# A perceiver stack on one core: products of the second attention in three reduced-precision passes, with changes to its loads, to a block inversion and to the self-attention

## The reference

```python
x = x + _L0_xattn_ref(...)  # attention over the context with a bias, 16 heads, then a feed-forward
x = x + _L0_attn_ref(...)   # delta-rule memory: per head and chunk of 64 the inverse of a unit triangular matrix
x = x + _L0_ffn_ref(...)    # eight dense gated experts, all of them summed
x = x + _L1_xattn_ref(...)  # second attention over the context, 16 heads of 64
x = x + _L1_attn_ref(...)   # self-attention over 64 tokens, 16 heads of 16
x = x + _L1_ffn_ref(...)    # eight experts, one picked per token
```

```python
q = x @ Wq
kv = context @ Wkv
k, v = jnp.split(kv, 2, axis=-1)
...
sim = jnp.einsum('bhid,bhjd->bhij', q, k) * scale
sim = jnp.where(mask[None, None, :, :], sim, max_neg)   # j % n_q == i: 16 of 1024 keys for each query
attn = jax.nn.softmax(sim, axis=-1)
out = jnp.einsum('bhij,bhjd->bhid', attn, v)
```

## Time and profile before

| what | value |
|---|---|
| median of 3 runs | 879.33 us (878.36 to 882.39) |
| the profiled execution's own time | 886.54 us |
| its span, first to last instruction | 884.7 us |
| mean granted TensorE clock | 0.986 |
| TensorE busy, matmuls | 832.1 us, 94% |
| VectorE busy | 511.5 us, 58% |
| ScalarE busy | 414.7 us, 47% |
| GpSimd busy | 97.4 us, 11% |

### The profile page before, as it was taken

How to read it: one execution, slowest core, us unless ns; L and a number is a source line. 1 busy time by engine, 2 the same in 40 slices (tenths; PEclk the granted TensorE clock), 3 DMA queues, 4 the chain that set the end, 5 groups by cost and what they waited for, 6 DMA issues and landing times.

```text
span 884.7 us, 20345 instructions
## 1 busy us (share of the span) xinstructions
PE 832.1 (94%) x8172; PEld 671.4 (76%) x8172; DVE 511.5 (58%) x1226; ACT 414.7 (47%) x852; POOL 97.4 (11%) x96
## 2 busy tenths in 40 slices
PE   7999999999889798999999999999998899879997
PEld 5888888888747796888888888887368757668785
DVE  6777887777646646555555555555246524575332
ACT  4666656666652224445445454443456632522221
POOL 1323320340000520000000000000000000400100
PEclk9999999999999799999999999999999999899999
DMA  8445654485090000123113213003617768033960
GB/s 315 178 138 202 235 213 159 135 285 199 5 399 1 3 4 2 43 101 142 69 75 142 86 57 142 0 0 141 239 49 282 282 248 333 1 147 115 367 235 25
DMA packets 26017, 128.19 MB, mean 145 GB/s; under 512 B 2376, under 2 KB 8416, under 8 KB 21856
## 3 DMA queue, kind: packets, MB, share of 16 engines
q1 hardware_dynamic: 24624, 110.83, 33.7%
q0 software_dynamic: 1328, 16.41, 4.8%
HBM read 126.71 MB, written 0.52 MB: 144 GB/s over the span
## 4 chain that ended last, share of the span: by engine, by line
PE 78%; DVE 9%; DMA 7%; issue 3%; ACT 2%; SPq 1%; DVEq 0%
PE PS L461 13%; PE PS L463 13%; PE PS L462 13%; PE PS L766 4%; PE PS L1220 3%; DMA arena<-in_bias 3%; PE PS L887 3%; PE PS L1232 3%; DMA hT<-in_ctxD 3%; PE PS L778 3%; PE PS L755 3%; PE PS L1034 2%; PE PS L481 2%; PE PS L1000 2%; PE PS L355 2%
## 5 line engine op out<-in xcount | busy, mean ns | idle before, releaser
L1401 ACT CAST w_h<-arena 128x768 fp32r<-128x768 f32 x64 | 53.4, 835 | 124.8 <-PE PS L463 124.8
L1755 DVE TENSOR_TENSOR w_l<-arena,w_h 128x768 fp32r<-128x768 f32 x64 | 61.2, 958 | 87.1 <-ACT w_h L1401 87.0
L461 PE MATMUL PS<-xnT_h,w_h 128*128 128x512 f32 x256 | 99.7, 389 | 1.4 <-DVE xnT_l L455 1.4
L463 PE MATMUL PS<-xnT_h,w_l 128*128 128x512 f32 x256 | 99.6, 389 | 0.0
L462 PE MATMUL PS<-xnT_l,w_h 128*128 128x512 f32 x256 | 99.6, 389 | 0.0
L1600 DVE CUSTOM_DVE_ANT_0 arena<-PS,arena 128x512 f32<-128x512 f32 x128 | 86.9, 715 | 19.9 <-PE PS L755 17.8
L1299 ACT ACTIVATE arena<-arena 128x1024 f32<-128x1024 f32 x64 | 73.5, 1150 | 10.8 <-DVE arena L1600 10.7
L766 PE MATMUL PS<-consts,arena 128*128 128x128 f32 x512 | 68.3, 277 | 0.7 <-ACT arena L1304 0.4
L766 PEld LDWEIGHTS PS<-consts,arena 128*128 128x128 f32 x512 | 55.9, 141 | 10.5 <-issue 3.6
L1762 DVE TENSOR_TENSOR arena<-PS,arena 128x512 f32<-128x512 f32 x64 | 44.3, 692 | 29.0 <-PE PS L463 27.3
L461 PEld LDWEIGHTS PS<-xnT_h,w_h 128*128 128x128 f32 x256 | 48.1, 188 | 11.6 <-DVE xnT_l L455 1.8
(11 more groups left out here) (312 smaller groups left out, 1736.0 us busy)
## 6 DMA issues: line engine op xcount, KB each, us to landing
arena<-in_bias SPq DMA_DIRECT2D x64, 512.0 KB, 4.1
arena<-in_wall SPq DMA_DIRECT2D x8, 3072.0 KB, 10.5
arena<-in_wf SPq DMA_DIRECT2D x8, 2052.0 KB, 11.2
hT<-in_ctxT SPq DMA_DIRECT2D x8, 1024.0 KB, 5.7
arena<-in_ctxD SPq DMA_DIRECT2D x4, 1024.0 KB, 7.6
arena<-in_ctxG SPq DMA_DIRECT2D x4, 1024.0 KB, 4.7
hT<-in_ctxD SPq DMA_DIRECT2D x4, 1024.0 KB, 8.2
hT<-in_ctxG SPq DMA_DIRECT2D x4, 1024.0 KB, 4.9
```

Of the source, the lines that this page charges most:

```text
L461: pe.matmul(out, a[0], b[0], start=start, stop=False)
L463: return pe.matmul(out, a[1], b[0], start=False, stop=stop)
L1401: act.copy(w_h[:, s % 4, :], stage[s // 8 % 2][:, s % 8, :]).then_inc(sem("c_wh"), 1)
L1755: dve.tensor_tensor(w_l[:, s % 4, :], stage[s // 8 % 2][:, s % 8, :], wide(w_h[:, s % 4, :]), ALU.subtract).then_inc(sem("c_wl"), 1)
```

## The change

The change merges several edits.

1. **Second attention.** Query weights and key weights are loaded while the dense experts still run, and GpSimd splits them (eight instructions). The normalised tokens are split on arrival. Queries and `U` are formed in three fp32r passes; ScalarE writes `qs_h`, VectorE the new `qs_l`.
2. **Contexts.** Three buffers instead of two. `wv1` and `wo1` are loaded after `U` is complete, ahead of context 3; the self-attention's weights and the last block's first five expert blocks after the product with `wv1` (before: earlier). The warming matmuls ahead of the batch loop go from 8 to 2.
3. **Inversion.** VectorE makes `T`, `MT` and `CT[1]` for two heads at a time; `TT` comes from TensorE (a product with the identity) and a ScalarE copy; GpSimd keeps the later masks alone.
4. **Self-attention.** The values of the second four batches are formed behind the first two tiles' scores; ScalarE takes over one of two value copies of VectorE and its last turned copy; `weighted` uses one bank for each tile, and `output` divides tile by tile.

```diff
+            w_in(wq1, A["wq1"], "in_wq1")
+            w_in(wkT1, A["wkT1"], "in_wq1")
 
             sp.wait_ge(sem("c_dn"), 4 + 8 * NEXP)
-            w_in(wq1, A["wq1"], "in_wq1")
-            w_in(wkT1, A["wkT1"], "in_wk1")
-            w_in(wv1, A["wv1"], "in_wvo1")
-            w_in(wo1, A["wo1"], "in_wvo1")
             for b in range(B):
-                if b >= 2:
-                    sp.wait_ge(sem("d_sim"), 2 * (b - 1))
...
+                if b == 3:
+                    for dc in range(KC):
+                        sp.wait_ge(sem(f"d_u{dc}"), 2 * FC)
+                    w_in(wv1, A["wv1"], "in_wvo1")
+                    w_in(wo1, A["wo1"], "in_wvo1")
+                if b >= 3:
+                    sp.wait_ge(sem("d_sim"), 2 * (b - 2))
+                sp.dma_start(ctxT1[b % 3], A["ctxD"][b].rearrange("(k p) n -> p k n", p=P))\
+                  .then_inc(sem(f"d_ctxT{b % 3}"), 16)
+                if b >= 3:
+                    sp.wait_ge(sem("d_w"), 4 * (b - 2))
+                sp.dma_start(ctxG[b % 3], A["ctxG"][b]).then_inc(sem(f"d_ctxG{b % 3}"), 16)
+            sp.wait_ge(sem("d_o"), FC)
             w_in(wqkv, A["wqkv"], "in_wqkv")
             w_in(wproj, A["wproj"], "in_wqkv")
...
-            for h in range(MH):
-                pool.wait_ge(sem("b_t"), h + 1)
-                pool.tensor_tensor(TT[:, h], MT[:, h], masked("up0"), ALU.mult).then_inc(sem("b_pool"), 1)
-                pool.wait_ge(sem("b_pool"), 2 * h + 1)
-                pool.tensor_tensor(TT[:, h], masked("pick64"), TT[:, h], ALU.subtract).then_inc(sem("b_pool"), 1)
+            pool.wait_ge(sem("b_ct"), MH)
...
+            pool.wait_ge(sem("in_wq1"), 32)
+            n = 0
+            for raw, high, low in ((wq1, wq1_h, wq1_l), (wkT1, wkT_h, wkT_l)):
+                half = raw.shape[1] // 2
+                for k in (slice(0, half), slice(half, 2 * half)):
+                    pool.tensor_copy(high[:, k], raw[:, k]).then_inc(sem("d_ws"), 1)
+                    n += 2
+                    pool.wait_ge(sem("d_ws"), n - 1)
+                    pool.tensor_tensor(low[:, k], raw[:, k], wide(high[:, k]), ALU.subtract).then_inc(sem("d_ws"), 1)
...
                     if k == 1:
+                        pe.wait_ge(sem("b_copied"), 3 + h)
+                        for t in range(NT):
+                            for r in halves:
+                                last = pe.matmul(PS[r, 4 + h, t * S:(t + 1) * S], T[r, h, t, :], C("pick64")[r],
+                                                 start=True, stop=True)
+                        last.then_inc(sem("b_x"), 1)
                         pe.wait_ge(sem("b_ct"), h + 1)
...
+            pe.wait_ge(sem("tr_l"), 4 * KC)
+            pe.wait_ge(sem("d_ws"), 4)
 
             def q_mm(c):
                 if c >= 2:
-                    pe.wait_ge(sem("d_qs"), c - 1)
+                    pe.wait_ge(sem("d_ql"), c - 1)
                 for ki in range(KC):
-                    last = pe.matmul(bank(c % 2), wq1[:, ki, c * P:(c + 1) * P], xnT[:, ki],
-                                     start=ki == 0, stop=ki == KC - 1)
+                    w = slice(c * P, (c + 1) * P)
+                    last = mm3(pe, bank(c % 2), (wq1_h[:, ki, w], wq1_l[:, ki, w]), (xnT_h[:, ki], xnT_l[:, ki]),
+                               ki == 0, ki == KC - 1)
...
                 for dc in range(KC):
-                    for h2 in range(2):
-                        if c:
-                            pe.wait_ge(sem(f"d_ue{dc}"), 2 * (c - 1) + h2 + 1)
-                        r = slice(64 * h2, 64 * h2 + 64)
-                        pe.matmul(bank(2 + 2 * h2 + dc), wkT1[r, c, dc * P:(dc + 1) * P], qs1[r, c % 2, :],
-                                  start=True, stop=True).then_inc(sem(f"d_u{dc}"), 1)
+                    if c:
+                        pe.wait_ge(sem(f"d_ue{dc}"), 2 * c)
+                    for n, (w, q) in enumerate(((wkT_h, qs_h), (wkT_h, qs_l), (wkT_l, qs_h))):
+                        for h2, r in enumerate(halves):
+                            last = pe.matmul(bank(2 + 2 * h2 + dc), w[r, c, dc * P:(dc + 1) * P], q[r, c % 2, :],
+                                             start=n == 0, stop=n == 2)
...
-            warm(pe, 7, 8)
+            warm(pe, 7, 2)
...
-            for h in range(MH):
-                dve.wait_ge(sem("b_gram"), 4 * (h // 2) + 1 + h % 2)
-                ch.add(dve.tensor_tensor(T[:, h], blocks(h), tiles(low0g[:, h, :]), ALU.mult))
...
+                ch.add(dve.tensor_tensor(T[:, two_heads], grams, per_head(low0g), ALU.mult))
+                ch.step(dve.tensor_tensor(MT[:, two_heads], grams, per_head(decayed), ALU.mult))
+                dve.tensor_tensor(per_tile(T), mask("pick64"), per_tile(T), ALU.subtract).then_inc(sem("b_t"), 2)
+                dve.tensor_tensor(per_tile(CT[1]), per_tile(MT), mask("up1"), ALU.mult).then_inc(sem("b_ct"), 2)
...
+            def queries_low(c):
+                dve.wait_ge(sem("d_qs"), c + 1)
+                dve.scalar_tensor_tensor(qs_l[:, c % 2, :], bank(c % 2), XD ** -0.5, wide(qs_h[:, c % 2, :]),
+                                         ALU.mult, ALU.subtract).then_inc(sem("d_ql"), 1)
+
+            queries_low(0)
             for c in range(FC):
+                if c + 1 < FC:
+                    queries_low(c + 1)
                 for h2 in range(2):
...
+            for t in range(NT):
+                output(t)
             dve.wait_ge(sem("e_yown"), 8)
```

More of the change, by code:

```diff
@@ L1106, in _ @@
             scores(1)
+            values(1)
             pe.wait_ge(sem("e_vsb"), 4)
@@ L1510, in _ @@
             turned(2)
-            act.wait_ge(sem("e_t"), 7)
-            act.copy(PT[:, 3, 0:4, :].rearrange("p a b -> p (a b)"), bank(6)).then_inc(sem("e_te3"), 1)
+            turned(3)
             for t in range(NT):
```

166 lines of the change are left out of this document (84 added, 82 removed).

## The result

| kernel | median, us | runs, us | ratio to the kernel before, 95% interval |
|---|---|---|---|
| before | 880.54 | 878.36 to 882.39 (4) | |
| changed | 860.96 | 859.70 to 861.62 (4) | 0.977, 0.9745 to 0.9795 |

The change takes 19.6 us, 2.3%. The forecast was 860.5 us. The profiled execution of the changed kernel took 860.73 us, so it lies on its median; that of the kernel before lay 6 us above its own. The pair of profiles therefore differs by 25.8 us in span, and some of that is not the change's. I come back to it, since it is the first trap here.

The account below looks back on a forecast made before the run. TensorE, busy 832.1 of 884.7 us, was taken to bound the kernel. The terms -2.5 + 1.5 - 5.1 - 2.7 - 4.6 - 5.4 = -18.8 us took 879.3 to 860.5 us, range 855 to 868.

Parts of the forecast that it names:

- A: Inversion: merged VectorE instructions end 2.0 us earlier, GpSimd no longer holds them up; -2.5 us (-3.6 to -0.3).
- B: Dense experts: GpSimd's weight split beside them delays VectorE's two-SBUF-input instructions; +1.5 us (0 to +3.4).
- C: Second attention's query loop: queries and U in fp32r passes, 2.92 instead of 3.83 us per pair of heads; -5.1 us.
- D: Warming ahead of the second attention's batch loop: 12 of 16 trace instructions go; -2.7 us (-2.7 to -2.0).
- E: Second attention's batches: a third context buffer removes the waits of sims for transfers; -4.6 us (-4.6 to -3.0).
- F: Self-attention: scores no longer wait for the second half of the values, output divides by tile; -5.4 us (-6.0 to -4.0).
- If the clock stays at 1.00 ... -3.6: Inversion, level 1: the stretch at a lower clock, worth 1.6 us, doesn't come, besides 2.0 from VectorE.
- casts hold it too: Experts: GpSimd casts as well as subtractions hold VectorE; the cycle is 5.08 us against a 4.08 us step, +3.4 us.
- at once: Experts, if casts hold VectorE too: 0.34 us late immediately, then 1.0 us in each of three further steps.
- Rival 2: Query loop: the two row halves don't run side by side in fp32r, a turn takes 4.28 us; 869 us, 6%.
- Rivals 1, 3 and 4: GpSimd keeps ports for series (5%, 874 us); batch loop transfer-bound (7%, 865 us); split late (2%, 889 us).
- Rival 5: A at its weak end and half of F lost because TensorE's clock falls to 0.50 in shorter gaps; 865 us, 10%.

Follow-up runs that it names:

- after_again: The changed kernel, unchanged, run and profiled once more: 860.55 us, ratio 0.9776 to the kernel before.
- vals_first: Changed kernel with both halves of the self-attention's values ahead of the first two tiles' scores again: 864.44 us, ratio 0.9812.
- split_x3: Changed kernel with GpSimd's weight split done three times beside the experts (12 casts, 12 subtractions instead of 4 and 4): 865.02 us, ratio 0.9829.
- u_pairs: Changed kernel with the query loop as two queries, then two U products, and three pairs of PSUM banks for U: 859.39 us.

## Why the prediction was right, and where its terms were not

860.5 was forecast and 860.96 measured, inside the range. The mechanisms were largely the ones named, but the hit on half a microsecond is luck: four terms were off by 1.2 to 1.5 us, two to either side, and the errors cancel.

| term | forecast | measured (stage) |
|---|---|---|
| A | -2.5 (-3.6 to -0.3) | -3.7 (-3.3 to -4.9 alone) |
| B | +1.5 (0 to +3.4) | 0.0 |
| C | -5.1 (-6.0 to -3.5) | -3.6 |
| D and E | -7.3 | -7.3 |
| F | -5.4 (-6.0 to -4.0) | -3.9 |
| sum | -18.8 | -18.5 |

**A** was right in mechanism and too small in size. VectorE ended 2.0 us earlier, as worked out (eight instructions from 293.85 to 299.13, sixteen from 293.77 to 301.05). "If the clock stays at 1.00 ... -3.6" was the case that came, in every profile; I took a value short of it because four products were added. They fell into gaps; that by filling them they helped to keep the clock up is likely but not shown, as no run has VectorE's part of the edit without them. What I could not see was that the first profile was 1.6 us slower there than the second; against the mean of both, the mean of twelve is -3.6.

**B**: "casts hold it too", the case priced at +3.4, is what the rows show. The price was wrong: I added the four durations to a round of 5.08 us, but the measured round is 4.54, since the start of one side lies under the end of the other. The 0.34 us "at once" were wrong too: `w_l` never waited for a whole subtraction, and its lateness grew evenly from nothing. With 0.46 us per round instead of 1.0, four rounds stay inside the slack. The split ran from 545.2 to 563.2 us, 18.0 us for durations of 13.7. The trial with twelve shows the same mechanism costing 3.6 us.

**C**: the step that failed is "the change between full and row-tiled matmuls cost about 0.1 us each time". It is 0.1 us at each of two starts, 0.2 in all: 3.16 us for a turn instead of 2.92, over seven turns 1.7 us, which accounts for the miss of 1.5. The second late start already stood in the trace of before, in the first attention (101.77 to 102.11 us, 0.34). Rival 2, halves of the rows one after another, did not happen: two 64-row products share one pass of 0.23 us.

**D and E** came as worked out: their sum is the forecast one. Undoing D alone costs more than it was forecast to give (3.4 us in the stage for 2.7), and its undone version has waits that the changed kernel hasn't. Undoing E costs 5.4 us in the median, 4.0 by the ratios, for a forecast of 4.6.

**F** was right about the start (VectorE's first maximum at 10.2 us behind the first query/key product instead of 11.9) and wrong about the size and part of the reason. From the first query/key product VectorE's last product of the output ends at 30.2 us, where the forecast has 29.7 and the first profile of before 35.2: 0.5 us of the miss. The rest is behind it, from there to the first expert product: 19.7 instead of 18.9 us, where the forecast had no difference. And the output by tiles, for which I counted 8.8 us of divisions from an earlier start, gives nothing; the copy taken from between the two divisions gives 2.8. Small slips of the recorded sum change nothing: its own rule for a reciprocal gives 1.71 us for 256 columns, not the 1.76 written (and measured), and its times give 4.7 for E and 5.5 for F.

Rivals 1, 3 and 4 (ports kept for a whole series, transfers still the bound, a late split) show nothing of themselves. Rival 5, the clock, occurs in small and in some executions: of the eight with an unedited changed self-attention, four kept 1.00 throughout the stage and took 48.5 to 49.2 us, four fell to 0.50 in it once or twice and took 49.8 to 50.2. In all three of the kernel before it fell twice. So about 1 us of F goes with the clock; what decides between the two cases was not tested.

What stays open: the last block's 4.8 us in one execution; the spread of the times of either kernel (877.8 to 885 us for the one of before), which follows the mean granted clock in some sets of runs (in `after_again` from 859.44 us at 0.999 to 862.49 at 0.992) and not in others; and the 2 us or so by which `vals_first` lies above what its stage shows.

## What to carry to other kernels

A second profile of the *unchanged* kernel costs one run and tells which of its stages move by themselves: here the last block moved by 4.8 us and the inversion by 1.6, together as much as any single term. Two are still few: the self-attention of before took 54.1 and 52.6 us, which looks as if the first were the odd one, and a third execution took 54.4. A term is read from a stage with fixed landmarks in both kernels, and undone alone before it is believed: the sum was right with four of five terms off by more than 1 us.

Work on GpSimd beside a bound TensorE was free here as long as the lateness that it gave VectorE, 0.46 us per round times the number of rounds, stayed under the 2.05 us of slack that the step has. Measure the round, don't add the durations.

Of an engine's queue ask what stands between two long instructions: one copy of 0.68 us between two divisions cost 2.8 us, while halving the divisions gave nothing.

## What the hardware showed that I had not expected

- A VectorE instruction with two SBUF inputs and a GpSimd cast exclude each other, and both are stretched: `h_l` 0.69 to 1.52 us, the cast 1.04 to 1.65, the subtraction 2.39 to 2.74, in a strict alternation of 4.54 us (`split_x3`).
- A change between full and row-tiled matmuls costs 0.1 us at each of two starts (about 0.33 instead of 0.23 us), in both directions, with nothing left to wait for (`u_pairs`, 620.75 and 623.98). A wait that ends just ahead of a start shows the same pair (623.08).
- In level 1 of the inversion TensorE stood for 0.67 to 1.23 us between stretches of 0.64 to 1.04 us of work in two executions of two, and fell to the 1.2 GHz level (0.50), which ended at 307.5 and at 306.1 us. Twelve executions whose waits there were 0.83 us and less stayed at 2.4 GHz (1.00) from 300 to 312 us.
